# Feature interaction on one core: four adjacent output rows in each partition, batches in column halves, transposes as quarter products

## What is computed

```python
bilinear = jnp.einsum('bie,ied->bid', feature, weight)
out = jnp.einsum('bid,bjd->bij', bilinear, feature)
```

## Time and profile before

| | |
|---|---|
| median of 3 runs | 1306.28 us (1301.26 to 1307.94) |
| the profiled execution | 1306.27 us |
| its span in the trace | 1304.5 us |
| HBM read, written | 108.13 MB, 327.68 MB |
| TensorE / VectorE / ScalarE / POOL busy | 92% / 71% / 81% / 19% of the span |
| granted TensorE clock, mean | 0.987 of 2.4 GHz |

### The profile page before, as it was taken

How to read it: one execution, slowest core, us unless ns; L and a number is a source line. 1 busy time by engine, 2 the same in 40 slices (tenths; PEclk the granted TensorE clock), 3 DMA queues, 4 the chain that set the end, 5 groups by cost and what they waited for, 6 DMA issues and landing times.

```text
span 1304.5 us, 56312 instructions
## 1 busy us (share of the span) xinstructions
PE 1198.4 (92%) x24384; PEld 1030.4 (79%) x24384; DVE 925.6 (71%) x1792; ACT 1056.7 (81%) x1185; POOL 247.1 (19%) x375
## 2 busy tenths in 40 slices
PE   5999999999989999999989989899998999889985
PEld 4788788887778878897778878788777887778864
DVE  0477677777777768677776777777766777677795
ACT  4898787987889877997879977799787987779964
POOL 2111111122211112111121211212121112111111
PEclk9999999999999999999999999999998999999998
DMA  9699999999999999999999999999999999999899
GB/s 243 208 354 358 335 339 345 356 348 363 325 349 347 357 347 344 345 354 351 347 351 337 335 325 347 357 354 330 360 351 316 347 325 345 322 341 347 311 345 318
DMA packets 266133, 439.58 MB, mean 337 GB/s; under 512 B 40608, under 2 KB 237216, under 8 KB 265888
## 3 DMA queue, kind: packets, MB, share of 16 engines
q1 hardware_dynamic: 222112, 317.90, 69.6%
q0 software_dynamic: 43776, 118.09, 28.4%
HBM read 108.13 MB, written 327.68 MB: 334 GB/s over the span
## 4 chain that ended last, share of the span: by engine, by line
PE 66%; DMA 14%; issue 6%; DVE 5%; ACT 5%; SPq 2%; ACTq 0%; POOLq 0%; DVEq 0%
PE ps L286 43%; DMA out_dram<-staging 12%; PE ps L255 12%; PE ps L268 11%; ACT staging L316 3%; DVE staging L316 2%; SPq L189 2%; DMA x<-feature_dram 2%; ACT bl L338 2%; DVE win L363 2%; DVE win L371 1%; DMA w<-weight_dram 1%; DVE win L370 1%; ACT xt L328 0%; SPq L179 0%
## 5 line engine op out<-in xcount | busy, mean ns | idle before, releaser
L286 PE MATMUL ps<-win,bl 64*64 64x200 f32 x16384 | 840.2, 339 | 60.1 <-ACT staging L316 35.3
L286 PEld LDWEIGHTS ps<-win,bl 64*64 64x64 f32 x16384 | 674.5, 175 | 152.4 <-issue 58.8
L316 ACT COPY staging<-ps 128x800 f32<-128x800 f32 x768 | 625.8, 868 | 164.9 <-PE ps L286 67.6
L316 DVE COPY staging<-ps 128x800 f32<-128x800 f32 x256 | 253.2, 989 | 207.8 <-PE ps L286 206.4
L363 DVE COPY win<-xt 128x400 f32<-128x400 f32 x512 | 282.9, 553 | 138.5 <-ACT xt L328 78.0
L338 ACT COPY bl<-ps 128x1024 f32<-128x1024 f32 (+1 forms) x208 | 305.1, 1467 | 36.8 <-PE ps L268 35.3
L231 POOL DMA_DIRECT2D out_dram<-staging x256 | 161.6, 631 | 890.5 <-DVE staging L316 541.9
L268 PE MATMUL ps<-xt,w 64*64 64x128 f32 x6400 | 235.8, 275 | 13.8 <-issue 12.0
L255 PE MATMUL ps<-ident,x 128*128 128x128 f32 x1600 | 224.3, 283 | 21.4 <-DMA x<-feature_dram 15.5
L328 ACT COPY xt<-ps 128x1024 f32<-128x1024 f32 (+1 forms) x208 | 212.1, 1020 | 36.6 <-PE ps L255 36.2
L255 PEld LDWEIGHTS ps<-ident,x 128*128 128x128 f32 x1600 | 175.1, 143 | 73.5 <-issue 65.5
(11 more groups left out here) (2 smaller groups left out, 0.2 us busy)
## 6 DMA issues: line engine op xcount, KB each, us to landing
out_dram<-staging SPq DMA_DIRECT2D x768, 400.0 KB, 6.3
x<-feature_dram POOLq DMA_DIRECT2D x96, 1024.0 KB, 8.9
out_dram<-staging POOLq DMA_DIRECT2D x256, 50.0 KB, 5.8
x<-feature_dram POOLq DMA_DIRECT2D x16, 256.0 KB, 5.8
w<-weight_dram SPq DMA_DIRECT2D x24, 128.0 KB, 6.8
w<-weight_dram SPq DMA_DIRECT2D x2, 64.0 KB, 6.2
```

Source lines behind the costliest of these rows:

```text
L286: last = nc.tensor.matmul(tile[64 * g:64 * g + 64, h ^ g, F * b:F * (b + 1)], lines_of_bl(n, h, g, R * ORDER[s // 2] + r), win[64 * h:64 * ...
L316: copy(staging[:, slot, PB * s % OCT:PB * s % OCT + PB].rearrange("p b h j -> p h b j"), tile_of("s", n, s)[:, :, 0:PB * F].rearrange("p h ...
```

## The change

- Set s of a block is now the elements 2s and 2s + 1. An output partition holds a quad, four adjacent output rows (fields 4k to 4k + 3) of one element: the first 64 partitions are one element, the other 64 the next. Of each 64 places 50 are used. Rows in stores have 3200 bytes, and `staging` holds four sets of one such row in a slot.
- SP still stores 96 partitions in three DMAs of 32; POOL stores the four others as two DMAs of two partitions.
- A line is transposed as four float32 products with 64x64 quarters of the identity, in two PSUM banks. x is loaded as one run of 2048 floats a partition.
- Bilinear products go by groups of three quads (six lines), 17 groups a block. The four quad places of a PSUM tile, one of them unused, are copied to `bl` whole, in one copy for 15 groups, in two and three pieces for the two groups with odd places. In an odd block the lines of a group lie next to each other in `bl`, in an even one the elements of a line.
- Half of the moving operands of the scores read `win` in swapped pairs; the bilinear products read `xt` with the even elements first, then the odd.
- Transposes stand behind set 1, 5, 10 ... 55, bilinear groups behind set 5, 9, 13 ... 57, 59, 61 and 62. VectorE clears the PSUM tiles once at the start.

The core of the diff:

```diff
+    NW = FH // 6 + 1
+    SETS = NB // 2
-    OCT = 8
+    OCT = 4
-    ORDER = [8 * a + i for a in range(LINES // 8) for i in (0, 1, 4, 5, 2, 3, 6, 7)]
-    ORDER += list(range(LINES - 1, CELLS))
+    SPARE = (51, 55)
...
-    out_v = out.rearrange("b (m h) j -> m b (h j)", h=2)
+    out_v = out.rearrange("(s g) (k r) j -> (g k) s (r j)", g=2, r=4)
...
+    def quads_of(j):
+        if j == NW - 3:
+            return [0, 1]
+        first = 3 * (j - (j >= NW - 3)) + 2
+        return [first, first + 1, first + 2]
+    def positions(g, k):
+        k -= 2 * (1 - g)
+        return 4 * (k // 3) + k % 3 if 0 <= k < 48 else SPARE[k % 48 if k >= 48 else k + 2]
+    def pieces(j):
+        if j == NW - 3:
+            return [(0, 1, 0, 2), (1, 1, 0, 2)]
+        if j == NW - 1:
+            return [(0, 1, 0, 3), (1, 1, 0, 1), (1, 1, 2, 2)]
+        return [(0, 2, 0, 4)]
...
-    transposed_at = {60 * u // NG + 2: u for u in range(NG)}
-    weighed_at = {s + 3: u for s, u in transposed_at.items()}
+    transposed_at = {59 * u // NG + 1: u for u in range(NG)}
+    weighed_at = {sets_before(j) - 1 if j != NW - 3 else 59: j for j in range(NW)}
...
-            return xt[:, t, :, c, :] if n % 2 == 0 else xt[:, :, t, c, :]
+            line = xt[:, t, :, c, :] if n % 2 == 0 else xt[:, :, t, c, :]
+            return line.rearrange("p k (s g) -> p g k s", g=2)
...
+        def features_of_win(q, half, r):
+            first = win[64 * half:64 * half + 64, q % WSLOTS, r, half:F]
+            if half == 0:
+                return first
+            return bass.AP(first.tensor, first.offset, [first.ap[0], [2, F // 2], [-1, 2]])
...
-                    sp.dma_start(out_v[Z * z:Z * (z + 1), b:b + OCT, :],
-                                 staging[z:128:4, slot].rearrange("p b h j -> p b (h j)")
+                    sp.dma_start(out_v[2 + z:2 + z + 3 * 31 + 1:3, OCT * q:OCT * q + OCT, :],
+                                 staging[z:128:4, slot].rearrange("p s i h j -> p s (i h j)")
...
-                    nc.gpsimd.dma_start(x[:, at % XSLOTS], halves[:, u // 2, u % 2]).then_inc(x_loaded[at % XSLOTS], 16)
+                nc.gpsimd.dma_start(x[:, at % XSLOTS, 0:size],
+                                    feature_v[n * NB:(n + 1) * NB, first:first + size]
...
+                for g in range(2):
+                    nc.gpsimd.dma_start(out_v[98 * g:98 * g + 2, OCT * q:OCT * q + OCT, :],
+                                        staging[64 * g + SPARE[0]:64 * g + SPARE[1] + 1:4, slot
...
-                        last = nc.tensor.transpose(transpose_tile(n, u)[:, g, :, c, :],
-                                                   x[:, at % XSLOTS, g, fs], ident[:])
+                        for a in range(2):
+                            for v in range(2):
+                                to = 64 * (a ^ v)
+                                h = a ^ v ^ c % 2
+                                e = 2 * E * (C * (2 * (u % 2) + g) + c) + E * h
+                                last = nc.tensor.matmul(transpose_tile(n, u)[to:to + 64, v, :, g, c, :],
+                                                        x[64 * v:64 * v + 64, at % XSLOTS, e:e + E],
+                                                        ident[64 * v:64 * v + 64, 64 * v:64 * v + 64],
+                                                        start=True, stop=True)
...
-                            last = nc.tensor.matmul(tile[64 * g:64 * g + 64, h ^ g, F * b:F * (b + 1)],
-                                                    lines_of_bl(n, h, g, R * ORDER[s // 2] + r),
-                                                    win[64 * h:64 * h + 64, q % WSLOTS, r, 1 - h:1 - h + F],
+                            last = nc.tensor.matmul(tile[64 * g:64 * g + 64, h, F * i:F * (i + 1)],
+                                                    lines_of_bl(n, h, g, i, s),
+                                                    features_of_win(q, h, 2 * (s % 2) + g),
...
-                nc.scalar.copy(group_of_bl(n, u).rearrange(at), weighed.rearrange(at)).then_inc(bl_stored, 1)
+                for piece in pieces(j):
+                    last = nc.scalar.copy(piece_of_bl(n, j, piece), piece_of_tile(n, j, piece))
+                last.then_inc(bl_stored, 1)
...
+            for tile in ps:
+                nc.vector.memset(tile[:], 0.0).then_inc(psum_cleared, 1)
```

More of the change, by code:

```diff
@@ L53, in quads_before @@
-    def quads_before(u):
-        return max(ORDER.index(t) for t in cells_of(u)) + 1
-    transposed_at = {60 * u // NG + 2: u for u in range(NG)}
-    weighed_at = {s + 3: u for s, u in transposed_at.items()}
[L59 to L67, removed]
+        return [2 * u + 1, 2 * u + 2] if u < NG - 1 else [0]
@@ new lines, in transposed_before, with needed, sets_before @@
+    def transposed_before(j):
+        def needed(j):
+            if j < 0:
+                return 0
+            u = (2 * quads_of(j)[-1] + 1 - C) // (2 * C)
+            return min(u + 2, NG) if 0 <= u and j < NW - 3 else NG
+        return range(needed(j - 1), needed(j))
+    def quads_before(u):
+        return max(cells_of(u)) + 1
+    def sets_before(j):
+        return max(positions(g, k) for k in quads_of(j) for g in range(2)) + 1
+    transposed_at = {59 * u // NG + 1: u for u in range(NG)}
@@ new lines, in feature_interaction @@
+    weighed_at = {sets_before(j) - 1 if j != NW - 3 else 59: j for j in range(NW)}
+    assert len(transposed_at) == NG and len(weighed_at) == NW and max(weighed_at) < SETS
+    assert list(weighed_at) == sorted(weighed_at)
+    assert all(s + 1 >= sets_before(j) for s, j in weighed_at.items())
+    for t, u in transposed_at.items():
+        for s, j in weighed_at.items():
+            lines = [2 * k + i for k in quads_of(j) for i in range(2)]
+            assert t < s or not any(m // C in cells_of(u) for m in lines)
@@ L68, in feature_interaction @@
+    fillings = []
+    for j in range(NW):
+        fillings += [("t", 0, u) for u in transposed_before(j)] + [("b", 0, j)]
     for n in range(BLOCKS):
-        for s in range(SETS_B):
+        for s in range(SETS):
             fillings.append(("s", n, s))
@@ L138, in quad_of_xt, with steps_of_bl @@
             return xt[:, 0:LINES, k, :, :] if n % 2 == 0 else xt[:, k, 0:LINES, :, :]
[L140 to L150, removed]
-            return bl[half, places, at] if n % 2 == 0 else bl[half, at, places]
+        def steps_of_bl(n):
+            return (NB, 1) if n % 2 == 0 else (1, NB)
@@ new lines, in piece_of_bl @@
+        def piece_of_bl(n, j, piece):
+            g, halves, slot, quads = piece
+            line, batch = steps_of_bl(n)
+            at = [dict(zip(slots(gg, j), (positions(gg, k) for k in quads_of(j)))) for gg in range(2)]
+            pos = at[g][slot]
+            step = at[g][slots(g, j)[-1]] - at[g][slots(g, j)[-2]] if quads > 1 else 1
+            for gg in range(g, g + halves):
+                for k, p in at[gg].items():
+                    assert not slot <= k < slot + quads or p == at[gg][slot] + step * (k - slot)
+            first = bl[:, 0, 0]
+            i = [64 * line, 2]
+            half = [64 * batch + (at[1][slot] - pos) * line if halves > 1 else 1, halves]
+            quad = [step * line, quads]
+            sets = [batch, SETS]
+            return bass.AP(first.tensor, first.offset + pos * line + 64 * g * batch,
+                           [first.ap[0]] + ([i, half, quad, sets] if n % 2 == 0 else [half, sets, i, quad]))
@@ new lines, in piece_of_tile, with lines_of_bl @@
+        def piece_of_tile(n, j, piece):
+            g, halves, slot, quads = piece
+            weighed = bilinear_tile(n, j)[:, :, g:g + halves, slot:slot + quads, :]
+            return weighed if n % 2 == 0 else weighed.rearrange("p i g k s -> p g s i k")
+        def lines_of_bl(n, r, g, i, s):
+            half = slice(64 * r, 64 * r + 64)
+            places = slice(64 * i, 64 * i + 64)
+            at = 64 * g + s
+            return bl[half, places, at] if n % 2 == 0 else bl[half, at, places]
```

189 lines of the change are left out of this document (94 added, 95 removed).

## The result

The changed kernel took **1564.03 us** (median of four runs, 1547.43 to 1570.52) beside 1304.69 for the kernel before on the same chip: a ratio of 1.197, 95% interval 1.187 to 1.207. It is slower by a fifth where 1254 us was forecast. The profiled execution took 1570.52 us with a span of 1568.6.

What follows compares the result with a forecast made beforehand. DMA was taken as the bound, 1291.5 us per engine: 1291.5 - 60 - 8 + 8 + 6 = 1237.5, at 99.0% busy a span of 1250, plus 2 for the boundary and 1.8 outside the span: 1254 us; range 1218 to 1325.

Steps and rivals of the forecast that it cites:

- The fetch of instructions: Fetching 22,400 more instructions for the quarter transposes, priced as DMA work: 5 to 6 us per engine, 6 taken.
- present 99.0%: Last step of the sum: the DMA engines stay 99.0% busy, so 1237.5 us of work gives a span of 1250.
- The work forecast: DMA work per engine after the change: 1291.5 - 60 - 8 + 8 + 6 = 1237.5 us.
- DMA is the bound, TensorE stands close behind it: Opening step: DMA engines 99.0% busy; TensorE needs 69.2 of a block's 77.6 us, with 8 to spare.
- Loads of x: Loading x in rows of 8192 bytes, not twice 4096: 0 to 11 us per engine saved, 8 taken.
- The boundary: Last lines weighed behind set 62 of 64 stop TensorE: 21 to 37 us uncovered, 2 taken as stores cover it.
- The stores: SP's stores in rows of 3200 bytes halve 196,608 packets: up to 85 us per engine saved, 60 taken.
- The odd weighed lines: ScalarE's copies of weighed lines in an odd block: 16.8 to 32.6 us, 18 taken.
- The transposes' pace: Quarter products at 55 ns a pass, 110 a line, 11.0 us a block for 14.8; TensorE's block falls from 69.2 to 65.4.
- The one on the slower side: Rival: quarter products cannot be paced at 55 ns; at 27 ns each 1320 us, at 133 ns 1395; chance 0.16.
- By the byte: Rival: DMA engines pay by the byte, so longer store and load rows save nothing: 1309 us; chance 0.11.
- odd lines stay dear: Rival: ScalarE's copies in odd blocks still cost 32.6 us, with waits 82 us a block: 1310 us; chance 0.11.

## Why the prediction was wrong

**The fetch of instructions, the step that failed.** The term "22,400 more (40%) add 5 to 6 us per engine. I take 6" priced the packets as DMA work alone. That part is right: 1.2% of 1568.6 for 1.0% of 1304.5, 6 us. What it left out is the one who waits for them. TensorE stands until the next 256 instructions are there, and with 71,168 of them in place of 48,768 it stood 292 us in stops above 0.7 us, and its granted clock fell with the stops. The price by the runs is 3.0 us a packet in the old kernel (281 packets) and, on top of the other losses of the change, 213 us for 88, 2.4 each, the clock included. The rows read could have raised it: the earlier trace rows showed how few the packets were and how little of the engines they took, and I read their small share as a small cost. The trace of before even held 19 stops, 24 us, that end behind such a packet; the prediction passed over them.

**The "present 99.0%" of the sum, the second failure.** The work forecast, 1237.5 us per engine, was near: 1231 with the old transposes (91.2% of 1349.8), 1256 with the quarters. But dividing it by 0.990 took for granted that the engines stay full. Without the quarters the sum would still have missed, 1351 for 1254. Of these 97 us the runs place about half: the loads of x 42 and the late copies 6 to 14. The trace of that run shows where the engines stood: in the four stages named above (sets 0 to 7, 8 to 47, 48 to 55, 56 to 63) their shares average 0.66, 0.96, 0.82 and 0.99, so of 6.9 us that they idle in a block 4.8 lie in the two stages in which TensorE's own pace holds. "DMA is the bound, TensorE stands close behind it" was true with 8 us a block between them, and half of that was what the change took from DMA.

**Loads of x.** "I take 8" as a gain, ends 0 to 11; 8192-byte rows cost 13 us, and another 29 can be had by halving the load, a lever that the kernel before does not have. The bounds looked at the fixed part of a packet only, and not at the stores, whose landing ScalarE awaited 35 us less beside the smaller loads. The Trainium skill (DMA: Bandwidth & Descriptors, section "Bandwidth") advises transfers of at least 1 MiB for three quarters of the peak; here two of 512 KB were worth 29 us more than one of 1024 KB, beside stores that others wait for.

**The boundary.** 2 us, as covered by stores, 21 to 37 uncovered. In the changed kernel TensorE waited 12.6 us for these copies (15 times, at most 2.0). Late copies cost 7 us in the old kernel, and 6 to 14 us came back where VectorE made those of the last two groups. The bounds held. The 36 us of other waits at the block's end are for stores, in a stage whose engines are full (0.99).

**What was right.** The stores: 60 forecast, 70 measured in SP's share, with the packets at 123,840 for the 124,000 named. The odd weighed lines, in windows of line 432 alone, the block that writes even and the one that writes odd, which answer to the earlier trace rows:

```profile
738.10:834.10 96.00, 16.99 (x20) 0.96 0.81 283
834.10:929.90 95.80, 19.56 (x20) 0.95 0.81 288
```

19.6 us for the 18 taken, where 32.6 was the dear end. The rule of the Trainium skill (SBUF — State Buffer, "Door 1: The DMA port swizzle") agrees in kind: with runs of four elements the odd copies cost 1.15 times the even ones, no longer 1.94 times. The transposes' pace: 0.88 us forecast for eight lines, 0.92 measured, but TensorE's block without stops was probably not 65.4 us, though no run shows it with quarters: by the run with cut stores, which has the old transposes (14.8 for 11.0 us), it was 71.6, the stop at its end included, against a reckoned 69.2.

**The rivals.** The one on the slower side had the sign and not the mechanism: quarters are paced at 14 ns, far under the 27 it priced. The Trainium skill (TensorE: Matmul & The Clock Gate, "Wait — 56ns, not 53.3ns?") has 25 ns as the floor between starts; the row of 0.92 us for 64 products does not bear that out for products on different quarters. The rival's words "128 more instructions in each group to be fetched through full DMA engines" held the cause, named as an argument and given no price of its own (the count is 112: 128 instructions for 16). "By the byte" and "odd lines stay dear" fell.

## What to carry to other kernels

Count the instructions of the busiest engine as well as its time: an edit that makes four or eight short instructions of one has to be paid in packets of 256, and where the DMA engines are full, each cost 3 us here, a lower clock after the stops included, though all of them together took 1% of the engines. When two resources are within a few per cent of each other, take the slower one stage by stage, not the larger sum; a saving on one then shows only in the stages it sets. And a load that shares engines with stores on which a staging ring waits can be better issued in smaller pieces: two halves gained 29 us where the engines had 7% of their time left, and nothing where they had 1%.

## What was not expected of the hardware

A packet of 256 instructions came every 5.4 us (median) beside 80% busy DMA engines and every 4.3 us beside 50% busy ones, so 21 or 17 ns an instruction, with TensorE standing for the next packet in both; the instructions themselves can run faster: 128 of them, 64 products and their loads, in 0.92 us, 7 ns each. Quarter products of 64 columns on four different quarters start 14 ns apart on the mean of such a stretch. And the stops cost twice: 42 of 43 stretches at TensorE's lower clock began in a stop above 0.7 us or within 2 us of its end.
